# Gate projections of an mLSTM layer: a narrow stationary, two batches per matmul, and another order of the steps around them

## The reference, cut to what matters

```python
h_in = _rmsnorm(x, norm1_w)
i_pre = _soft_cap(h_in @ w_ig + b_ig)      # 15 * tanh(. / 15), 8 heads
f_pre = _soft_cap(h_in @ w_fg + b_fg)
Fcum = jnp.cumsum(jax.nn.log_sigmoid(f_pre), axis=-1)
Dmat = Fcum[..., :, None] - Fcum[..., None, :] + i_pre[..., None, :]   # causal
m = jnp.max(Dmat, axis=-1, keepdims=True)
C = (q @ k.T / sqrt(16)) * jnp.exp(Dmat - m)
h = (C / jnp.maximum(jnp.abs(jnp.sum(C, -1)), jnp.exp(-m))) @ v
```

## Time and profile before

| what | value |
|---|---|
| median of 3 runs | 673.22 us (672.23 to 675.36) |
| profiled execution | 672.34 us, span 670.6 us |
| TensorE busy | 658.1 us (98% of the span), 5297 matmuls |
| VectorE, ScalarE, GpSimd busy | 438.3, 411.3, 246.7 us |
| mean granted TensorE clock | 0.995 |
| projections of the mLSTM | from 473.76 to 502.9 us |
| heads | from 502.9 to about 541 us |

### The profile page before, as it was taken

One profiled execution on the slowest core, in us unless ns is written; L12 is line 12 of the kernel. 1 busy time (PEld: TensorE's weight loads), 2 busy tenths in 40 slices (PEclk: granted clock), 3 DMA queues, 4 the chain that ended last, 5 costly groups with the idle time before them and its releaser, 6 DMA issues. The chain is left out here.

```text
span 670.6 us, 15275 instructions
## 1 busy us (share of the span) xinstructions
PE 658.1 (98%) x5297; PEld 633.0 (94%) x5297; DVE 438.3 (65%) x968; ACT 411.3 (61%) x1085; POOL 246.7 (37%) x279
## 2 busy tenths in 40 slices
PE   8999999999999999999999999999999999999995
PEld 8999999999999999999999899999987799999995
DVE  6556557557666655765665576556569986556877
ACT  5556677666776666866577773334689864333553
POOL 3731972134353133632328555112451462222011
PEclk9999999999999999999999999999999899999999
DMA  7174654435534436534363404000166100000000
GB/s 254 37 219 160 193 172 140 133 101 174 168 127 113 127 108 185 161 128 126 97 183 124 111 1 151 32 0 2 48 208 243 65 1 1 1 1 0 1 33 31
DMA packets 38172, 69.74 MB, mean 104 GB/s; under 512 B 3440, under 2 KB 22640, under 8 KB 37872
## 3 DMA queue, kind: packets, MB, share of 16 engines
q1 hardware_dynamic: 37696, 68.38, 32.8%
q10 hardware_dynamic: 432, 0.79, 0.4%
HBM read 52.18 MB, written 16.97 MB: 103 GB/s over the span
## 5 line engine op out<-in xcount | busy, mean ns | idle before, releaser
L312 PE MATMUL PJ<-xTh,WBh 128*128 128x256 f32 x364 | 106.7, 293 | 0.3 <-POOL WBl L839 0.3
L314 PE MATMUL PJ<-xTh,WBl 128*128 128x256 f32 x364 | 103.0, 283 | 0.0
L313 PE MATMUL PJ<-xTl,WBh 128*128 128x256 f32 x364 | 102.8, 283 | 0.0
L824 POOL TENSOR_TENSOR stage<-stage 128x256 f32<-128x256 f32 x32 | 24.5, 766 | 165.0 <-DVE stage L691 165.0
L584 ACT ACTIVATE probs<-probs,rinv 128x256 f32<-128x256 f32 x128 | 58.4, 507 | 26.7 <-DVE rinv L707 26.7
L1202 PE MATMUL UG<-xTh,WBh 128*128 (+1 forms) x256 | 73.6, 288 | 0.3 <-PEq L54 0.3
L1205 PE MATMUL UG<-xTh,WBl 128*128 (+1 forms) x256 | 72.4, 283 | 0.0
L1203 PE MATMUL UG<-xTl,WBh 128*128 (+1 forms) x256 | 72.4, 283 | 0.0
L1274 ACT ACTIVATE ga<-UG 128x256 f32<-128x256 f32 x64 | 24.5, 383 | 75.1 <-PE UG L1205 75.1
L312 PEld LDWEIGHTS PJ<-xTh,WBh 128*128 128x128 f32 x364 | 69.6, 191 | 0.9 <-issue 0.5
L313 PEld LDWEIGHTS PJ<-xTl,WBh 128*128 128x128 f32 x364 | 69.6, 191 | 0.0
(11 more groups left out here) (320 smaller groups left out, 2385.9 us busy)
## 6 DMA issues: line engine op xcount, KB each, us to landing
K<-scr_k SPq DMA_DIRECT2D x60, 256.0 KB, 4.3
raw<-in_w_att SPq DMA_DIRECT2D x37, 256.0 KB, 4.7
Q<-scr_q SPq DMA_DIRECT2D x15, 512.0 KB, 7.5
stage<-scr_m SPq DMA_DIRECT2D x6, 768.0 KB, 5.9
scr_q<-rot_h SPq DMA_DIRECT2D x30, 128.0 KB
scr_q<-rot_l SPq DMA_DIRECT2D x30, 128.0 KB
scr_k<-rot_h SPq DMA_DIRECT2D x30, 128.0 KB
scr_k<-rot_l SPq DMA_DIRECT2D x30, 128.0 KB
```

Of the source, the lines that this page charges most:

```text
L312: pe.matmul(out, ah, bh, start=(i == 0), stop=False)
L313: pe.matmul(out, ah, bl, start=False, stop=False)
L314: last = pe.matmul(out, al, bh, start=False, stop=(i == n - 1))
L824: pool.tensor_tensor(y[:, 0:S], c[:, 0:S], sn[:, S:2 * S], ALU.subtract).then_inc(rope_sum, 1)
```

## The change

Both kinds of gates now lie in one stationary of 64 columns (input gate in 0 to 31, forget gate in 32 to 63), without padding. The gates of batches 0 and 1 are one group of six matmuls that move 512 columns into one bank; batches 2 and 3 are six matmuls of 256 columns each. The tanh of each batch and kind (8 activations on 32 partitions instead of 2 on 128) moves the rows to partitions 32c. The order on TensorE, ScalarE and VectorE is another: the gates of batches 0 to 2 stand inside the projection of batch 0, those of batch 3 inside q and k of batch 1; the steps of batch 3's norm are interleaved with the evacuations of batch 0; tanh, exp and log stand earlier on ScalarE; two MLP pieces (10, 11) are rounded in the heads stage of batch 0, and their two transfers are issued after those of `m_first`.

The function `project_part(c, i, which)` is `project_qk` for q (i = 0) or k (i = 1) and for a choice of its two halves; `project_vog(c, t)` does one of the two row tiles. `gates_exp` and `gates_log` are the last two activations of `gates`, in the same form. The heading lines in the diff name the engine.

```diff
-        gate_w = WI[:, :, :].rearrange("p a n -> p (a n)")[:, 12 * PIECE - 4 * KT * WIDE:]
...
+        gate_w = WI[:, 11, PIECE - 4 * KT * 32:].rearrange("p (l t n) -> p l t n", l=2, t=KT)
+        WGh, WGl = gate_w[:, 0], gate_w[:, 1]
+        WG_parts = [gate_w[:, l].rearrange("p t (g n) -> p t g n", g=2) for l in range(2)]
-        wg_f = stage1[:, 0:2 * KT * WIDE].rearrange("p (t g n) -> p t g n", t=KT, g=2)
+        wg_f = stage1[:, 0:2 * KT * WIDE].rearrange("p (t g n) -> p t g n", t=KT, g=2)[:, :, :, 96:128]
-        gate_sums = (X[:, 0:S], OUTS[:, 1, 0:S])
+        gate_sums = [bank[0:2 * 32, i * S:(i + 1) * S] for bank in (X[:, :], OUTS[:, 1, :]) for i in range(2)]
# sync
-            more(RING, 12)
+            more(RING, 10)
...
                 m_first(quarter)
+            more(10, 12)
# tensor
-            def project_gates(c):
+            def project_gates(c, n=1):
-                pe.wait_ge(s_["xt_split"], N_T[1] + c + 1)
+                pe.wait_ge(s_["xt_split"], N_T[1] + c + n)
...
-                w = slice(96 - 32 * c, 96 - 32 * c + P)
-                for n, out in enumerate(gate_sums):
-                    for i in range(3 * KT):
-                        t, (a, b) = i // 3, ((WGh, xh_v), (WGh, xl_v), (WGl, xh_v))[i % 3]
-                        last = pe.matmul(out, a[:, t, n, w], b[:, t, c, :], start=(c == 0 and i == 0),
-                                         stop=(c == B - 1 and i == 3 * KT - 1))
+                if c == B - 1:
+                    pe.wait_ge(s_["gates_tanh"], B - 1)
+                out = X[0:2 * 32, :] if n == 2 else gate_sums[c]
+                for t in range(KT):
+                    for i, (w, x) in enumerate(((WGh, xh_v), (WGh, xl_v), (WGl, xh_v))):
+                        last = pe.matmul(out, w[:, t, :], x[:, t, c:c + n, :], start=(t == 0 and i == 0),
+                                         stop=(t == KT - 1 and i == 2))
-            project(0)
-            for c in range(B - 2):
-                project_gates(c)
+            project_part(0, 0)
+            project_part(0, 1)
+            project_gates(0, 2)
+            project_vog(0, 0)
+            project_gates(2)
+            project_vog(0, 1)
             pe_T(pe, 1, B - 1)
-            project_gates(B - 2)
-            project_qk(1)
-            project_gates(B - 1)
-            project_vog(1)
+            project_part(1, 0)
+            project_part(1, 1, range(1))
+            project_gates(3)
+            project_part(1, 1, range(1, 2))
+            project_vog(1, 0)
+            project_vog(1, 1)
             project(2)
# scalar
-            def gates():
-                act.wait_ge(s_["gates_ready"], B)
-                act.wait_ge(s_["bgs_ready"], 1)
+            def gates_tanh(c):
+                act.wait_ge(s_["gates_ready"], max(c, 1))
+                if c == 0:
+                    act.wait_ge(s_["bgs_ready"], 1)
                 for n in range(2):
-                    last = act.activation(gt[:, n, :], gate_sums[n], ACT.Tanh, scale=1.0 / CAP,
-                                          bias=bgs[:, n:n + 1])
+                    at = slice(32 * n, 32 * n + 32)
+                    last = act.activation(gt[32 * c:32 * c + 32, n, :], gate_sums[c][at, :], ACT.Tanh, scale=1.0 / CAP,
+                                          bias=bgs[at, n:n + 1])
                 last.then_inc(s_["gates_tanh"], 1)
...
-            mlp_hi(0, 5)
+            mlp_hi(0, 2)
+            evac_q(0)
+            mlp_hi(2, 3)
+            evac_k(0)
+            mlp_hi(3, 4)
             act_ssq(act, 1, 3)
-            evac_q(0)
-            evac_k(0)
+            for c in range(3):
+                gates_tanh(c)
+            act_hi(act, 1, 3)
             evac_og(0)
-            act_hi(act, 1, 3)
+            evac_q(1)
+            mlp_hi(4, 5)
+            gates_tanh(3)
+            gates_exp()
+            evac_k(1)
+            gates_log()
             mlp_hi(5, 6)
-            evac_q(1)
+            evac_og(1)
+            evac_q(2)
             mlp_hi(6, 7)
-            evac_k(1)
-            mlp_hi(7, 8)
-            gates()
-            evac_og(1)
-            mlp_hi(8, 9)
-            evac_q(2)
+            evac_k(2)
+            mlp_hi(7, 9)
+            evac_og(2)
             mlp_hi(9, 10)
-            evac_k(2)
-            mlp_hi(10, 12)
-            evac_og(2)
             exp_nm()
...
+                    if c == 0 and pair < 2:
+                        mlp_hi(10 + pair, 11 + pair)
# vector
             add_out(dve, 0, 3)
             dve_stats(dve, 1, 3)
+            split_q(0)
             dve_apply(dve, 1, 3)
+            split_k(0)
             dve_xs(dve, 1, 3)
-            split(0)
+            take_v(0, 0)
+            take_v(0, 1)
             dve_lo(dve, 1, 3)
             split(1)
             chain()
```

More of the change, by code:

```diff
@@ L961, in layers @@
         WI = sb("WI", [P, 12, PIECE], F32R)
-        gate_w = WI[:, :, :].rearrange("p a n -> p (a n)")[:, 12 * PIECE - 4 * KT * WIDE:]
-        WGh, WGl = (gate_w[:, i * 2 * KT * WIDE:(i + 1) * 2 * KT * WIDE].rearrange("p (t g n) -> p t g n", t=KT, g=2)
-                    for i in range(2))
+        gate_w = WI[:, 11, PIECE - 4 * KT * 32:].rearrange("p (l t n) -> p l t n", l=2, t=KT)
+        WGh, WGl = gate_w[:, 0], gate_w[:, 1]
+        WG_parts = [gate_w[:, l].rearrange("p t (g n) -> p t g n", g=2) for l in range(2)]
         raw = sb("raw2", [P, RING, PIECE])
@@ L1476, in project_gates, with project_part @@
+                out = X[0:2 * 32, :] if n == 2 else gate_sums[c]
[3 more added lines that the diff above has]
+                                         stop=(t == KT - 1 and i == 2))
                 last.then_inc(s_["gates_ready"], 1)
-            def project_qk(c):
+            def project_part(c, i, which=range(2)):
@@ L1480, in project_qk @@
                 if c == 0:
                     pe.wait_ge(s_["wl_split"], LP - 1)
[L1482 to L1488, removed]
-                    last.then_inc(s_["qk_ready"], 1)
@@ L1491, in project_vog @@
[L1491 to L1497, removed]
+                else:
+                    pe.wait_ge(s_["qk_split"], 2 * c - 1 + i)
@@ new lines, in project_part, with project_vog @@
+                for n in which:
+                    w = slice((2 * i + n) * P, (2 * i + n + 1) * P)
+                    last = six(UG[i][:, n * S:(n + 1) * S], [(WLh[:, t, w], WLl[:, t, w]) for t in range(KT)],
+                               x_parts(c))
+                if which[-1] == 1:
+                    last.then_inc(s_["qk_ready"], 1)
+            def project_vog(c, t):
+                if c:
+                    pe.wait_ge(s_["og_ready"], 2 * (c - 1) + t + 1)
+                rows = slice(t * P, (t + 1) * P)
+                six(UG[2 + t][:, :], [(xh_v[:, f, c, rows], xl_v[:, f, c, rows]) for f in range(KT)],
+                    [(WLh[:, 2 + f, :], WLl[:, 2 + f, :]) for f in range(KT)]).then_inc(s_["vog_ready"], 1)
@@ L1499, in project @@
             def project(c):
-                project_qk(c)
-                project_vog(c)
+                project_part(c, 0)
+                project_part(c, 1)
+                project_vog(c, 0)
+                project_vog(c, 1)
             def rows_T():
@@ L1647, in _ @@
             act.wait_ge(s_["wg_in"], 16)
-            act.activation(WGh, wg_f, ACT.Copy).then_inc(s_["wg_hi"], 1)
+            act.activation(WG_parts[0], wg_f, ACT.Copy).then_inc(s_["wg_hi"], 1)
             act.wait_ge(s_["small_in"], 16 * 4)
@@ L1667, in evac_og, with gates_exp, gates_log @@
                     act.activation(og_v[:, c, t, :], UG[2 + t][:, D:2 * D], ACT.Tanh, scale=0.5).then_inc(s_["og_ready"], 1)
-            def gates():
-                act.wait_ge(s_["gates_ready"], B)
-                act.wait_ge(s_["bgs_ready"], 1)
+            def gates_tanh(c):
+                act.wait_ge(s_["gates_ready"], max(c, 1))
+                if c == 0:
+                    act.wait_ge(s_["bgs_ready"], 1)
                 for n in range(2):
-                    last = act.activation(gt[:, n, :], gate_sums[n], ACT.Tanh, scale=1.0 / CAP,
-                                          bias=bgs[:, n:n + 1])
+                    at = slice(32 * n, 32 * n + 32)
+                    last = act.activation(gt[32 * c:32 * c + 32, n, :], gate_sums[c][at, :], ACT.Tanh, scale=1.0 / CAP,
+                                          bias=bgs[at, n:n + 1])
                 last.then_inc(s_["gates_tanh"], 1)
-                act.wait_ge(s_["gates_tanh"], 1)
+            def gates_exp():
+                act.wait_ge(s_["gates_tanh"], B)
                 act.activation(gt[:, 1, :], gt[:, 1, :], ACT.Exp, scale=-CAP).then_inc(s_["gates_tanh"], 1)
-                act.wait_ge(s_["gates_tanh"], 2)
+            def gates_log():
+                act.wait_ge(s_["gates_tanh"], B + 1)
                 act.activation(gt[:, 1, :], gt[:, 1, :], ACT.Ln, bias=1.0).then_inc(s_["sp_ready"], 1)
@@ L1823, in _ @@
             dve.wait_ge(s_["wg_hi"], 1)
```

(2 more changed lines are left out.)

## The result

The changed kernel takes 680.73 us (median of 4 runs, 679.21 to 682.07) against 672.91 us before: the ratio is 1.0109, 95% interval 1.0071 to 1.0147. I had forecast 670.6 us, 2.3 us less than before, and it became 7.8 us more. The profiled execution took 681.96 us with a span of 680.1 us.

The account below looks back on a forecast made before the run. TensorE was taken as the bound, full in the gates' stretch and nearly so early in the heads. 672.34 - 2.93 + 0.1 + 0.2 = 669.7 us, plus 0.88 for the median gives 670.6; range 668.4 to 673.0.

Parts of the forecast that it names:

- Fewer gate matmuls: Main term, TensorE in the projections: 48 gate matmuls of 5.74 us become 18 of 2.81 us, saving 2.93 us.
- The deadline of the last gates: Projections: TensorE waits for batch 3's norm, loss 0.1 us (0 to 0.5); as a rival 671.3 us, chance 0.08.
- Tanh, exp and log; the tables: ScalarE, projections: earlier order meets batch 1's output gate by 0.25 us; rival, 2.5 us late, 672.9 us, chance 0.08.
- The rows' way through DRAM: SyncE's queue: rows move 2.9 us sooner with the scans; pieces 10 and 11 ahead of batch 1's broadcasts cost 0.
- Two roundings in the heads: ScalarE, heads: 1.08 us more work in a nearly full stretch, loss taken as 0.2 us, bounds 0 and 1.08.
- The clock: Rival, heads: the one fall of TensorE's clock, worth 1.7 us, doesn't come; 668.9 us, chance 0.17.
- the other side: Rival, heads: ScalarE's 1.08 us reach TensorE and two more clock falls come; 674.9 us, chance 0.10.
- the heads lose more than the projections gain: Rival, heads: waits on ScalarE and two extra clock falls lose 4.5 us against 2.8 gained; 674.9 us, chance 0.10.

Follow-up runs that it names:

- e9: e8 with piece 11 rounded in the first pair of batch 2 and split by GpSimd only after the fourteenth mask; 669.82 us, ratio 0.9957.
- e7: Changed kernel plus eight useless 512-column matmuls ahead of the values of batch 0's last pair in the heads; 676.46 us, ratio 1.0066.
- e3: Changed kernel with GpSimd splitting only 8 of 512 columns of pieces 10 and 11; three runs 681.7 to 683.1 us, one 669.5.
- e10: e8 with GpSimd splitting only 8 of 512 columns of piece 11, ScalarE's rounding left in place; 669.78 us, ratio 0.9960.
- e6: Changed kernel with the transfers of pieces 10 and 11 queued behind batch 1's broadcasts instead of ahead; 680.27 us, ratio 1.0135.
- e2: Kernel before, with only pieces 10 and 11 fetched behind the rows' first broadcasts and rounded and split in batch 0 of the heads; 674.73 us, ratio 1.0036.
- e8: Changed kernel, MLP pieces reordered: piece 10 fetched ahead of the rows, rounded before the heads; piece 11 rounded in batch 0's third pair; 679.32 us.
- e11: Kernel before plus four useless 256-column VectorE operations ahead of the third pair of batch 0 of the heads; 684.45 us, ratio 1.0168.
- e4: Changed kernel with the transfers of pieces 10 and 11 moving only 8 of 512 columns; 670.89 us, ratio 0.9974.
- e1: Kernel before with only the 64-column stationary, the two-batch gate group and the eight tanhs, old order kept; 677.36 us, ratio 1.0063.
- e5: Changed kernel plus five useless 512-column matmuls where TensorE waited 1.11 us in batch 0 of the heads; 672.54 us, ratio 1.0002.

## Why the prediction was wrong

*Fewer gate matmuls, 2.93 us.* Right. Six of 512 columns from 476.99 to 478.37, 1.38 us as worked out; the six of batch 2 from 479.74 to 480.43, 0.69, and those of batch 3 from 484.40 to 485.09, 0.69, where I had 0.72. A 64-column stationary costs nothing extra. The projections shrank by 2.87 us. With the heads undisturbed the whole forecast comes out: 670.6 us was forecast for the change, and e9 measured 669.8.

*The deadline of the last gates.* Right: TensorE waited for neither the norm nor the three tanhs. `add_out` began at 474.31, 0.03 us after the recorded end of the FFN's last products (473.77 + 0.51), where before it had been 0.44; with the FFN's end 0.35 us later the norm came at the same time as before. The remainder of batch 3 was ready at 484.26, 0.14 us ahead of the last gates (484.40).

*Tanh, exp and log; the tables.* Met, but with nothing to spare. The timeline of ScalarE,

```profile
479.10 1.90 ACT L1684 ACTIVATE gt<-X,bgs 32x256 f32<-32x256 f32 x4
...
489.67 1.28 ACT L1675 ACT_TABLE_LOAD   x1
490.96 0.66 ACT L1675 ACTIVATE x<-UG 128x256 f32<-128x256 f32 x2
```

has the output gate's tanh of batch 1 right behind its table load (489.67 + 1.28 = 490.95), so again no drain was seen behind a load, which the Trainium skill has (ScalarE: Activation LUTs, What ACT_TABLE_LOAD costs); with its 1.38 us the output gate would, by my estimate, have been late by more than a microsecond. The first of the two ended at about 491.3 (a single one takes 0.38), 0.1 us ahead of TensorE's first matmul into that bank (491.43, recorded with 0.47 instead of 0.40, so it may have lost 0.07). My tanhs were priced at 0.94 a pair and took 0.94; only "some 2.4 us" for six more was too low against my own price, which gives 2.8.

*The rows' way through DRAM.* **This step failed.** I wrote that pieces 10 and 11 ahead of batch 1's broadcasts cost 0, because these are issued early. Three terms were wrong. The scans ended 1.4 us later than I had them (492.48 instead of 491.1), 1.0 of it through the collision at 489.89; so the first broadcasts went out at 494.09 instead of 492.7, and the four took 2.72 us to issue instead of 1.74 (in e7's profile they took 1.75, and the two pieces behind them 1.80 instead of 0.85); and batch 1's came at 497.81, later than before (497.42), while TensorE's need of them had moved 2.5 us ahead. The rows' slack of before was used up by the change itself, and the 0.5 MB in front of them did the rest: 0.78 us in the profile of the change, 1.89 in e3.

*Two roundings in the heads.* **This step failed too**, by looking at one engine. I followed ScalarE, whose load did no harm (e10), and left out that each rounding starts a split on GpSimd. I took 0.2 us; the two collisions took 0.95 and 0.64 us of VectorE, and TensorE waited 1.11. In the kernel before, the last splits ended at 499.26, ahead of the masks of batch 0 (500.14); in the change two of them fell onto the masks. A collision costs VectorE up to 1.1 us, and it has no such reserve. In this block the trace of before showed no collision: its splits ended at 491.14, ahead of the scans at 491.70, and ran again from 494.21 to 499.26. Further on it did show one, VectorE first, then GpSimd:

```profile
554.52 1.03 DVE L1330 TENSOR_TENSOR QKl<-gb,QKh 128x256 fp32r<-128x256 f32 x1
```

```profile
553.98 1.28 POOL L2072 TENSOR_TENSOR xres<-x,xres 128x512 f32<-128x512 f32 x1
```

The first takes 0.42 us elsewhere, and ends here 0.29 us after the second. The price could have been read there, and the rule of the Trainium skill named above would have said of which pairs to ask it. I had read 12.10 of 13.00 us busy for VectorE and then followed ScalarE alone.

*The clock.* **This term was too small by far.** I had a fall as a lottery of 1.7 us, and in the case of the other side two more of these: 674.9 at worst. The price was wrong by its kind. The fall of before lasted 3.4 us, from 520.9 to 524.3. It came in batch 2, where four transposes with 128 rows follow soon, and the clock was back 0.3 us behind their end:

```profile
523.02 1.06 PE L1561 MATMUL X<-ident,ho 128*128 128x128 f32 x4
```

So it was, within 0.3 us, in e9 (transposes from 520.50, back at 521.6) and e6 (from 528.41, back at 529.1); in the change, in e2, e3, e8 and e11 the clock didn't come back with those four, but within some 2 us of the output projection's twelve matmuls, two pairs later. A fall in batch 0 finds nothing but pairs until then, and lasted 20 to 31 us; in the change 15.4 us of lost clock and, with the pace of the pairs at 3.0 us instead of about 1.7, some 10 us of time. e7 shows that dense matmuls end it, and e11 that a late VectorE, with a wait of 0.64 us put in, starts it. The case "the heads lose more than the projections gain" was in the list, with a chance of 0.10, but with the wrong engine and little more than a third of the price (4.5 of 12.1 us). The range ended at 673.0, and should have reached as far as one fall in batch 0.

What stays open is what exactly brings a fall. By the waits in the one profile that each kernel has, 0.64 us (e11), 0.98 (e8), 1.11 (the change) and 1.92 (e6) went with a long fall in all four runs of each, 1.28 (e3) in three of four, 0.40 (e2, e4) in six of twenty; e9 and e10, with no wait over 0.38 in the heads, had none in 13. But the kernel before fell briefly behind a wait of 0.28 us (518.00), and e7 for long behind 0.22. So a wait makes the fall likelier and isn't its only condition, and in some executions of the change itself the fall may have come before the 1.11 us. e1 waited 4.5 us in the projections and had half clock for only some 3.4 us behind it (498.6 to 502.0), 1.7 us of lost clock. I have not tried waits of graded length.

## What to carry to other kernels

Before a step is moved into a stage, list for that stage every engine that the step wakes, not only the one that executes it, and ask what each of them does beside its neighbours there; here it was the split after the rounding and the transfer before it. Look in the trace at hand for a place where the same two engines already meet: the longer duration there is the price. Ask of every stage of thin matmuls what it would cost if the clock fell at its start: waits of 0.6 to 1.1 us went with a loss of some ten, and a few useless matmuls or, better, no collision gave it back. And where a stage is made shorter, work out anew the slack of all that has to arrive in the next one.

## What the runs showed of the hardware

- A VectorE operation with both inputs in SBUF nearly stood still during GpSimd's `tensor_tensor`: 1.63, 1.42 and 1.32 us instead of 0.68, 0.42 and 0.68, each ending 0.55 us (512 elements) or 0.28 us (256) after the split beside it. Where the VectorE operation began first, the split was the longer one: 1.74 instead of 1.28 us (e7). Operations with an operand in PSUM kept their time (1.01 us for two).
- An activation of 256 elements on 32 partitions with the bias from memory takes 0.47 us, as one on 128 partitions does; eight in a row took 3.78 us (e1), while of two on 128 partitions the second began 0.37 us behind the first (before).
- A weight load of 64 columns took 0.134 us instead of 0.19 (change), and the matmuls of 256 columns came 0.115 us apart instead of 0.1196.
- A fall of TensorE's clock to 1.2 GHz was kept through 30 us in which TensorE's busy time is the whole stretch (11.00, 10.00 and 8.00 us of the stretches 509 to 520, 520 to 530 and 530 to 538 of the change). The falls ended at or shortly behind eight matmuls of 512 columns in a row (e7), twelve of 256 (change, e2, e3, e8, e11) or four transposes (before, e6, e9).
- Waits of TensorE of 0.22 us (e7, 1.2 us ahead) and 0.28 us (before, 2.9 us ahead) were the only ones near a fall; waits of 0.22 to 0.40 us in e4, e5 and e10 came ahead of none.
